# Mixture-of-experts block: the long path for an expert's remaining rows, written as loops on TensorE

## The reference

```python
x = x + tanh(g_xattn[0]) * fp8_product(layernorm(x), ctx_2048)
x = x + tanh(g_ffn[0]) * moe(layernorm(x), Wg, w1, w2)

def moe(x, Wg, w1, w2):            # S = 2048 rows, E = 8 experts, top 2 of 8, C = 640
    probs = softmax(x @ Wg)
    gate_vals, expert_idx = top_k(probs, 2)
    # each expert takes its rows in order, at most C = 640 of them
    h = relu(dispatched @ w1)      # per expert: (640, 512) @ (512, 2048)
    expert_out = h @ w2            # per expert: (640, 2048) @ (2048, 512)
    return combine_weights . expert_out, back in the order of the rows
```

## Time and profile before

| what | value |
|---|---|
| median of 3 runs | 963.79 us (960.53 to 964.62) |
| profiled execution, its own time | 969.04 us |
| its span | 967.2 us |
| mean granted clock of TensorE | 0.946 |
| TensorE matmuls (PE) busy | 849.7 us, 88% of the span |
| VectorE busy | 681.6 us, 70% |
| ScalarE busy | 354.6 us, 37% |
| GpSimd busy | 198.0 us, 20% |
| TensorE on the chain that ended last | 75% of the span, "issue" 4% |

### The profile page before, as it was taken

The page is one execution under the profiler, slowest core; times in us unless marked ns, Lnnn a source line. Parts: engine busy times, 40 slices in busy tenths (PEclk is TensorE's granted clock), DMA queues, the critical chain, the costliest instruction groups (busy, mean ns, idle before and its releaser), DMA issues.

```text
span 967.2 us, 13282 instructions
## 1 busy us (share of the span) xinstructions
PE 849.7 (88%) x4733; PEld 409.1 (42%) x4734; DVE 681.6 (70%) x1155; ACT 354.6 (37%) x573; POOL 198.0 (20%) x167
## 2 busy tenths in 40 slices
PE   0486879659989999999999899999999899989987
PEld 0232347534434444444444334443444344434433
DVE  5999997778845888687788457846784768484530
ACT  4656766434240424244143404331342224133410
POOL 2231331050112113302320121022202220222010
PEclk9978877559999999999999999999999999999999
DMA  8500613245355437636543553354426442602000
GB/s 295 227 0 24 237 36 139 88 159 212 108 113 198 142 99 168 214 115 163 198 132 106 117 198 110 112 140 173 134 88 163 158 152 88 164 25 65 1 24 21
DMA packets 76739, 123.48 MB, mean 128 GB/s; under 512 B 40814, under 2 KB 40830, under 8 KB 72576
## 3 DMA queue, kind: packets, MB, share of 16 engines
q1 hardware_dynamic: 66976, 93.07, 29.5%
q0 software_dynamic: 9696, 29.39, 10.1%
HBM read 96.49 MB, written 18.87 MB: 119 GB/s over the span
## 4 chain that ended last, share of the span: by engine, by line
PE 75%; DVE 15%; issue 4%; ACT 3%; DMA 2%; POOL 1%; ACTq 0%; SPq 0%; DVEq 0%; POOLq 0%
PE mm L686 35%; PE mm L622 32%; DVE top L1090 2%; PE xT_ps L488 2%; PE mm L600 2%; DVE region L1020 2%; PE marks_ps L509 1%; PE mm L468 1%; DMA w_stage<-in_ctx 1%; DVE region L1016 1%; DVE region L995 1%; DVE region L984 1%; ACT region L913 1%; POOL region L396 1%; PE mm L478 1%
## 5 line engine op out<-in xcount | busy, mean ns | idle before, releaser
L686 PE MATMUL mm<-region,w_split 128*128 128x512 f16 x1536 | 349.6, 381 | 8.7 <-issue 8.7
L622 PE MATMUL mm<-region 128*128 128x512 f16 x1536 | 339.0, 381 | 16.5 <-DVE region L1294 13.1
L622 PEld LDWEIGHTS mm<-region 128*128 128x128 f16 x1536 | 148.9, 98 | 198.8 <-DVE region L1294 15.6
L686 PEld LDWEIGHTS mm<-region,w_split 128*128 128x128 f16 x1536 | 142.4, 98 | 169.0 <-issue 15.2
L902 ACT ACTIVATE region<-mm 128x512 f16<-128x512 f32 x128 | 76.4, 597 | 348.5 <-PE mm L686 340.6
L1281 DVE SCALAR_TENSOR_TENSOR region<-mm,region 128x512 f16<-128x512 f32 x128 | 88.5, 692 | 95.8 <-ACT region L902 93.1
L409 POOL DMA_INDIRECT out<-region,back_now x40 | 64.9, 1623 | 188.1 <-DVE region L1294 159.1
L1284 DVE SCALAR_TENSOR_TENSOR region<-w_stage,w_scale,region 128x512 f16<-128x512 f32 x128 | 96.4, 753 | 0.0
L905 ACT ACTIVATE region<-w_stage,w_scale 128x512 f16<-128x512 f32 x128 | 91.2, 712 | 0.0
L1086 DVE TENSOR_REDUCE top<-w_stage 128x1 f32<-128x512 f32 x128 | 85.9, 678 | 0.0
L386 POOL PARTITION_ALL_REDUCE peak_all<-peak x16 | 5.9, 372 | 372.7 <-DVE peak L1066 366.7
(11 more groups left out here) (169 smaller groups left out, 647.4 us busy)
## 6 DMA issues: line engine op xcount, KB each, us to landing
w_stage<-in_L_ffn_w SPq DMA_DIRECT2D x64, 1024.0 KB, 5.4
region<-in_x SPq DMA_DIRECT2D x4, 1024.0 KB, 14.2
x_split<-region SPq DMA_DIRECT2D x8, 512.0 KB, 3.3
out<-region SPq DMA_DIRECT2D x4, 1024.0 KB, 6.3
w_stage<-in_ctx SPq DMA_DIRECT2D x2, 1024.0 KB, 14.2
region<-in_ctx SPq DMA_DIRECT2D x2, 1024.0 KB, 16.2
region<-x_split,row_next POOLq DMA_INDIRECT x40, 5.2
region<-out,row_next POOLq DMA_INDIRECT x40, 4.1
```

Of the source, the lines that this page charges most:

```text
L622: mm = pe.matmul(mm2[s % 2][:, :], hidden[:, hh, f, s * P:(s + 1) * P], w2_split[:, wh, f, :], start=(f == 0 and hh + wh == 0), stop=(f == ...
L686: mm = pe.matmul(products(f), w1_split[:, wh, k, f * P:(f + 1) * P], xT[:, xh * KD + k, 0:WIDE], start=(k == 0 and wh + xh == 0), stop=(k ...
```

## The change

- `large_rest` on TensorE becomes loops. `first_rest` loops over `f` with 12 matmuls in the body, where 192 were written out; the last product loops over `f` with 3 matmuls of 128 stationary columns, where 192 matmuls of 32 stationary columns were written out. A small matmul at the end of each loop (`end_loop`) raises the semaphore.
- `hidden_rest` is laid out as half, `f`, piece, column, so that all four pieces of one `f` are one stationary operand of 128 columns. For piece 0 the values go first to `rest_rows`, the first 512 elements of each half, from where `turn_rows` reads them, and the turned values go to `hidden_rest[:, :, :, 0, :]`.
- ScalarE and VectorE keep the same instructions in number; the pieces 1 to 3, and the turned values of piece 0, are now written in runs of 32 elements with a stride of 128.

```diff
-        hidden_rest = cut(64, 8, F16).rearrange("p (h r f c) -> p h r f c", h=2, r=PARTS, f=NF)
+        hidden_rest = cut(64, 8, F16).rearrange("p (h f r c) -> p h f r c", h=2, r=PARTS, f=NF)
+        rest_rows = cut(64, 8, F16).rearrange("p (h n) -> p h n", h=2)[:, :, 0:NF * PART]
...
+        rest_idle = mm1[0][:, 0, 0:E]
...
+        rest_columns = cut(64, 8, F16).rearrange("p (h n) -> p h n", h=2)
+        w2_rows = cut(0, 32, F16).rearrange("p (h n) -> p h n", h=2)
+
+        def rest_piece(h, c):
+
+            if c == 0:
+                return rest_rows[:, h, :].rearrange("p (f c) -> p f c", f=NF)
+            return hidden_rest[:, h, :, c, :]
...
             def first_rest(c):
 
-                start = WIDE + PART * c
-                for f in range(NF):
+                with nc.tensor.Fori(0, NF) as f:
                     for k in range(KD):
                         for wh, xh in PASSES:
-                            mm = pe.matmul(rest1[:, f, :], w1_split[:, wh, k, f * P:(f + 1) * P],
-                                           xT[:, xh * KD + k, bass.ds(start, PART)],
-                                           start=(k == 0 and wh + xh == 0), stop=(k == KD - 1 and wh == 1))
-                return mm
+                            pe.matmul(rest1_flat[:, bass.ds(f * PART, PART)], w1_split[:, wh, k, bass.ds(f * P, P)],
+                                      xT[:, xh * KD + k, bass.ds(c * PART + WIDE, PART)],
+                                      start=(k == 0 and wh + xh == 0), stop=(k == KD - 1 and wh == 1))
+
+            def second_rest(f, first):
+
+                for hh, wh in PASSES:
+                    pe.matmul(rest2, rest_columns[:, hh, bass.ds(f * P, P)], w2_rows[:, wh, bass.ds(f * D, D)],
+                              start=(first and hh + wh == 0), stop=(hh == 1), skip_group_check=True)
...
-                        mm = pe.transpose(rest_turns[:, hh, j, :], hidden_rest[:, hh, 0, PARTS * j:PARTS * (j + 1), :].rearrange(
-                            "p f c -> p (f c)"), ident16[:, :])
+                        mm = pe.transpose(rest_turns[:, hh, j, :], rest_rows[:, hh, P * j:P * (j + 1)], ident16[:, :])
...
+            def end_loop(name):
+
+                pe.matmul(rest_idle, ident16[:, :], ones16[:, 0:E], start=True, stop=True).then_inc(q[name], 1)
...
-                            mm = pe.matmul(rest2[PART * g:PART * (g + 1), :], hidden_rest[:, hh, 0, f, :],
+                            mm = pe.matmul(rest2[PART * g:PART * (g + 1), :], hidden_rest[:, hh, f, 0, :],
...
             def large_rest(e, last):
                 with nc.tensor.Fori(1, PARTS) as c:
                     pe.wait_ge(q["rest_lo"], e * PARTS + c + 1)
-                    first_rest(c).then_inc(q["rest_more"], 1)
+                    alone(pe, q["pe_passed"])
+                    first_rest(c)
+                    end_loop("rest_more")
                 second(e, 1, last, NF // 2, NF)
                 pe.wait_ge(q["rest2_read"], e + 1)
                 pe.wait_ge(q["rest_lo"], e * PARTS + PARTS + 1)
-                for f in range(NF):
-                    for hh, wh in PASSES:
-                        for c in range(PARTS):
-                            mm = pe.matmul(rest2[PART * c:PART * (c + 1), :], hidden_rest[:, hh, c, f, :],
-                                           w2_split[:, wh, f, :], start=(f == 0 and hh + wh == 0),
-                                           stop=(f == NF - 1 and hh == 1))
-                mm.then_inc(q["rest2_done"], 1)
+                second_rest(0, True)
+                with nc.tensor.Fori(1, NF) as f:
+                    second_rest(f, False)
+                end_loop("rest2_done")
...
-                    nc.scalar.activation(hidden_rest[:, 0, c, :, :], rest1,
-                                         ACT.Relu).then_inc(q["rest_hi"], 1)
+                    nc.scalar.activation(rest_piece(0, c), rest1, ACT.Relu).then_inc(q["rest_hi"], 1)
...
-                                hidden_rest[:, hh, 0, :, :].rearrange("p (g j) c -> p g j c", g=PARTS),
+                                hidden_rest[:, hh, :, 0, :].rearrange("p (g j) c -> p g j c", g=PARTS),
...
-                    V.scalar_tensor_tensor(hidden_rest[:, 1, c, :, :], rest1, 0.0, hidden_rest[:, 0, c, :, :],
+                    V.scalar_tensor_tensor(rest_piece(1, c), rest1, 0.0, rest_piece(0, c),
                                            ALU.max, ALU.subtract).then_inc(q["rest_lo"], 1)
```

## The result

The changed kernel takes 926.99 us (median of 4 runs, 925.85 to 927.94); the kernel before, with one more run, 962.16 us. The ratio is 0.9624, with a 95% interval of 0.9597 to 0.9651: 35.2 us less. The forecast was 937, with a range of 931 to 948. The sign and the mechanism held; the size was too small by more than the range allows.

What follows compares the result with a forecast made beforehand. The prediction took TensorE's computing and its waits for code in the experts as the bound. Stalls of 13.1 and 8.7 us plus 4.9 of clock made 26.7, off 963.79: 937.1, said as 937 us, range 931 to 948.

Steps and rivals of the forecast that it cites:

- What bounds the kernel, and that the stalls are waits for code: TensorE in the experts: computing time plus ten stalls at jumps, taken as waits for instruction fetches, not for VectorE's `combine(1)`.
- Eight blocks held, the body 146 instructions short of the border: TensorE's code: eight blocks of 256 instructions held; the shortened loop body ends in A6, 146 instructions before its end.
- the prediction's rule: TensorE's fetches: each block, when entered, has the next one fetched; eight are held and the oldest is thrown out.
- second rival: "The way back still stalls": at the loop's return too many blocks are touched, so only 16.2 us gained, 947.6; chance 0.08.
- Points 1 to 3, the jumps and the way back: Shorter long path removes five stalls before `second(e, 2)`, 13.1 us, and four at the loop's return, 8.7 us.
- Point 4, the clock: TensorE after stalls: three falls of the clock to 0.50 cost 4.9 us; all taken as gained, 0 kept as bound.
- Point 5, expert 7: Jump after `no_rest` in expert 7 still exceeds one block; its 2.96 us stall left in place, bounds 0 and 2.96 gained.
- Point 6, `first_rows`: `first_rows` in five experts, 4.5 us against 2.8 in `small_rest`: given no gain; bound 1.7 us in four experts, 6.8.
- The sum's base: Gains subtracted from the median 963.79 us, which is 5.25 us less than the profiled execution's 969.04.
- more is gained: Rival: points 5 and 6 were fetches too, so 2.96 and 6.8 us more go, giving 927; chance 0.06.

Runs made afterwards that it cites:

- fourth chip: Kernel before against the unedited changed kernel, with gaps in `first_rows`: 972.12 us before, 939.36 changed, ratio 0.9660.
- second chip: Changed kernel rerun unedited against the kernel before, with gaps in `first_rows`: 937.04 us against 970.57, ratio 0.9645.
- third chip: Kernel before, unedited changed kernel and three edits of it, without gaps in `first_rows`: 960.35 us before, 925.04 changed in one run.
- the variant timed beside it: Changed kernel with the first 12 matmuls of `second(e, 1)` moved ahead of `first_rows`: 927.28 us, 0.9639 of the kernel before.
- fifth chip: Kernel before profiled once more beside the unedited changed kernel, with gaps in `first_rows`: 971.32 and 968.80 us before, 937.81 changed.

## Why the prediction missed, point by point

*What bounds the kernel, and that the stalls are waits for code*: right. The long code alone brings back 57 fetches and all of the time; dead instructions that pass the border bring back the stalls on the way back.

*Eight blocks held, the body 146 instructions short of the border*: right as far as tried. 64 instructions more changed nothing, 192 more took it past. In the changed kernel's expert 0 six packets come between 210 and 300 us; with the first block and the one after it, which by the prediction's rule were there before, that is eight, and no further one comes up to expert 7. The last of the six shows how far the body reaches:

```profile
q8 instruction: 1, 0.02, 6.0%
```

It comes between 288 and 289 us, at 288.8, when the last block is entered. The 13 us up to the way back are some 120 instructions (13.3 x 192 / 20.89), so about 135 are left to the border, where I had 146. The way back doesn't stall after the change. The Trainium skill, "Runtime: NRT & Kernel Launch", section "Instruction fetch mechanics", says that only two lines are held; this case's traces don't agree, with 549 us of a loop over six to eight blocks and not one fetch. Its 128 KiB and 16 KiB agree: 57 packets of 0.93 MB, and eight of them held. (The prediction calls what follows from the two lines its second rival; in its list it is the first.)

*Points 1 to 3, the jumps and the way back, 21.8 us*: right. Two pairs of profiles from one chip each: the kernel before has 25.3 and 24.7 us of idle time before L622 and L686, the changed one 0 and 0.3. Without expert 7's stall that is 22.6 and 21.4 us.

*Point 4, the clock, 4.9 us*: mis-sized. I took the number of falls from one execution. Five profiles of long code show how it varies, each with ten stalls: three falls behind a stall in the first, then four, four and three in the repeats of the kernel before, and five in the long code with the new layout, 1.4 to 1.8 us each. In the changed kernel's five profiles there is one from expert 1 on, where I foresaw none: on the fourth chip, in expert 4, behind a gap of `first_rows`.

```profile
625.25 0.49 PE L615 MATMUL mm<-w_split,region 128*32 128x512 f16 x3 [1.43 <-issue]
```

```profile
625.43:628.84 3.41, 3.41 (x11) 1.19 (x9) 0.69 (x1) 0.60 (x1) 0.00 (x0) 0.50 0.96 216
```

It cost 1.5 us (L636 is busy for 337.3 us instead of 335.8). So the term is 4.9 to 8.7 us by profiles. The sums close within about 1 us: on the second chip 25.3 + 6.6 = 31.9 for a distance of spans of 31.0; on the fourth 24.7 + 7.0, less the changed kernel's 1.5 and 0.3, is 29.9 for 31.1.

The timed runs may lose more. On the third chip the mean granted clock was 0.939 to 0.947 before and 0.951 to 0.954 in the variant timed beside it. If all time below full clock is at the lower level, (1 - 0.944) x 960 x 2 = 108 us against (1 - 0.954) x 927 x 2 = 85: 22 us more at the lower level, which is half of that in lost work, 11 us, or six falls. With 25 us of stalls that makes 36, and 33 to 35 was measured. This is argued from the clocks, and weakly: no profile shows six falls, and where falls can be counted the reckoning is off by 1 to 3 us. On the fifth chip (0.950 over 967.0 us, 0.957 over 936.0) it gives 8.1 us where the profile has three falls, some 5. Before 205 us, where no expert runs, the granted clock also varies from profile to profile (0.79 to 0.82).

*Point 5, expert 7*: wrong. I kept 2.96 us because the jump is longer than a block. What counts is in which block it ends. The trace before had the answer, in a row that the prediction doesn't use, the fetch queue from 933 to 934 us:

```profile
q8 instruction: 1, 0.02, 5.8%
```

`no_rest`'s last matmul ends 2.96 us before 939.61, at 936.65. So a border is crossed 3 us, some 28 instructions, before the jump. From there a jump of 440 instructions ends 468 behind the border: past the block just entered and in the one after it, which this packet brings. A jump of 1145 ends beyond that. The fetch queue of the changed kernel has a packet between 895 and 896 us and one between 898 and 899 us:

```profile
q8 instruction: 1, 0.02, 7.4%
```

```profile
q8 instruction: 1, 0.02, 8.3%
```

The first comes 3 us before `no_rest`'s last matmul ends, at about 898.7: the border had been crossed before the jump, and the target's block was fetched. None of the 15 profiles with short code has a stall there. The bound that I had written down, 2.96, was what came.

*Point 6, `first_rows`*: right that the change gives it nothing, though comparing the two first profiles says 9 us. The trace before came from a chip with gaps, the result from one without.

*The sum's base*: the median was 5.25 us less than the profiled execution, and I wrote "what it lacks lies in no part that I can name". Here was the sign. The kernel before took 968.8 to 970.9 us in its profiled executions with gaps, and 957.6 to 967.6 us in the timed runs on the third chip, where the kernels beside it had none. The profile was most likely of the one sort and the timed runs of the other. The gain itself is much alike on both: by medians 31 to 34 us on chips with gaps, 33 to 35 on those without.

The rival "more is gained" gave 927 and hit the number by luck: 2.96 of it came true, 6.8 for `first_rows` did not. The step that failed is the sum, in its points 4 and 5: 26.7 us where 29.7 stood in the trace, since expert 7's stall was put at nothing gained and went whole, and the clock's term was taken from one execution with three falls, where profiles show three to five. From 962.16 us, 21.8 of stalls, 2.96 of expert 7's and 4.9 to 8.7 of the clock lead to 928.7 to 932.5; 926.99 was measured. What makes up the last 1.7 to 5.5 us is open; six falls of the clock would do it, and no profile shows them.

## What to carry to other kernels

Count the blocks of code that one pass of a loop touches, jumped-over paths included, and keep them within what TensorE holds: code that never runs can cost as much as code that does, here 13.7 us for 192 dead instructions and 35 us of 962 in all. A wait at a jump that the profile gives to another engine is checked by its distance to that engine's end over several passes. And a stall costs more than its idle time when the clock falls behind it; how often that happens is not to be read from one execution.

## What the runs showed of the hardware

- TensorE kept eight blocks of 16 KB of instructions. With nine touched per pass (96 dead matmuls) a pass fetched all nine (experts 4 and 5), and the way back cost 2.0 to 2.2 us. In the five profiles of long code a jump forward to a block neither held nor asked for cost 2.3 to 3.3 us and the way back 2.0 to 3.1; a jump into a block just asked for cost 0.8 to 1.2 (96 dead matmuls).
- The 48 matmuls of `first_rows`, with 32 stationary columns, took 2.8 us in the result's profile and on the third chip, and 4.5 to 5.1 in the other profiles with the scatter and the order of products in place, mostly with gaps from the 42nd on; the changed kernel, unedited, showed both. 12 matmuls with full stationary operands in front removed the gaps on the fourth chip (939.36 to 928.70 us).
- After stalls of 2.0 to 3.3 us the clock fell to 0.50, the 1.2 GHz level, in 19 of 50 cases over five profiles of long code, and lost 1.4 to 1.8 us each time; once it fell behind a gap of 1.43 us. The first profile's rows are the earlier trace rows.
